# Building a pair-wise channel matrix with 64 block-diagonal products over 64 rows instead of 128 products over 16 rows

## The reference, cut to what matters

```python
def _L0_cond_ref(x, weights, condition):      # x (128, 64, 1024), weights (16, 64, 64)
    W = weights[condition]
    return jnp.einsum('bct,bcd->bdt', x, W)
...
x = x + _L0_cond_ref(x, L0_cond_weights, itok_B_0_15)
x = x + _L1_cond_ref(x, ..., itok_B_78_3631)   # long convolution along t, masked by a length
x = x + _L2_cond_ref(x, ..., itok_B_1_7)       # 1024x1024 linear layer along t, with adapters
x = x + _L3_cond_ref(x, ..., itok_B_8_3872)    # second long convolution
```

## Time and profile of the kernel before

| | us |
|---|---|
| median of 3 executions | 1711.64 (1707.01 to 1713.04) |
| the profiled execution | 1710.22 |
| its span in the trace | 1708.2 |
| PE busy | 1578.8 (92%) |
| first product of L561 | 10.79 |
| first product of stage 0 (L612) | 31.14 |

### The profile page before, as it was taken

One profiled execution on the slowest core, in us unless ns is written; L12 is line 12 of the kernel. 1 busy time (PEld: TensorE's weight loads), 2 busy tenths in 40 slices (PEclk: granted clock), 3 DMA queues, 4 the chain that ended last, 5 costly groups with the idle time before them and its releaser, 6 DMA issues.

```text
span 1708.2 us, 30846 instructions
## 1 busy us (share of the span) xinstructions
PE 1578.8 (92%) x12183; PEld 1033.3 (60%) x12183; DVE 1029.7 (60%) x1336; ACT 531.8 (31%) x674; POOL 826.4 (48%) x365
## 2 busy tenths in 40 slices
PE   6577774899999999999999999999999999999996
PEld 6576773365666656565657574747474747474744
DVE  6577766546575756565655656665656565656532
ACT  3444442323232323232323232323232323232211
POOL 2000006336556555656565656574747473838334
PEclk9888987899999999999999999999999999999998
DMA  4799994336263535353535252626252525252314
GB/s 120 195 334 368 356 342 159 74 48 160 48 147 60 140 66 135 71 135 71 135 70 136 61 145 52 149 47 148 58 140 66 140 66 140 66 128 74 79 50 99
DMA packets 433122, 216.80 MB, mean 127 GB/s; under 512 B 345336, under 2 KB 419584, under 8 KB 431040
## 3 DMA queue, kind: packets, MB, share of 16 engines
q1 hardware_dynamic: 413760, 204.19, 45.5%
q10 hardware_dynamic: 19328, 12.14, 2.5%
HBM read 94.19 MB, written 71.76 MB: 97 GB/s over the span
## 4 chain that ended last, share of the span: by engine, by line
PE 82%; DVE 6%; DMA 4%; issue 3%; SPq 2%; ACT 2%; ACTq 1%; POOL 0%; POOLq 0%; DVEq 0%
PE ps L730 39%; PE ps L765 7%; PE ps L668 7%; PE ps L695 6%; PE ps L722 5%; PE ps L738 5%; DMA arena<-in_x_dram 4%; PE ps L778 3%; PE ps L612 3%; PE ps L672 3%; PE ps L712 2%; PE ps L708 1%; SPq L352 1%; PE ps L561 1%; DVE arena L1462 1%
## 5 line engine op out<-in xcount | busy, mean ns | idle before, releaser
L730 PE MATMUL ps<-arena,w2t 128*128 128x512 f16 x3072 | 681.3, 379 | 0.0
L730 PEld LDWEIGHTS ps<-arena,w2t 128*128 128x128 f16 x3072 | 300.6, 98 | 362.5
L529 POOL TENSOR_TENSOR arena<-arena 128x1024 f32<-128x1024 f16 x64 | 152.8, 2387 | 545.8 <-DMA arena<-arena 528.2
L1468 DVE TENSOR_SCALAR arena<-ps,biasx 128x512 f32<-128x512 f32 x128 | 94.3, 747 | 214.6 <-ACT arena L1056 214.4
L1056 ACT ACTIVATE arena<-ps,biasx 128x512 f16<-128x512 f32 x128 | 87.3, 688 | 425.6 <-PE ps L738 425.6
L505 POOL TENSOR_TENSOR arena<-arena 128x1024 f32<-128x1024 f32 x32 | 73.7, 2305 | 288.6 <-DMA arena<-tab_scratch 261.3
L612 PE MATMUL ps<-arena 128*128 128x128 f32 x1024 | 150.2, 312 | 57.5 <-DMA arena<-in_x_dram 35.9
L612 PEld LDWEIGHTS ps<-arena 128*128 128x128 f32 x1024 | 141.3, 223 | 64.8 <-issue 33.8
L695 PE MATMUL ps<-arena 128*128 128x512 f16 (+1 forms) x768 | 138.7, 332 | 11.8 <-DVE arena L1389 9.4
L765 PE MATMUL ps<-arena 128*128 128x256 f16 (+1 forms) x1536 | 138.8, 247 | 3.2 <-DVE arena L1462 3.0
L532 POOL TENSOR_TENSOR arena<-arena,one_xs 128x1024 f32<-128x1024 f32 x64 | 136.1, 2126 | 5.0
(11 more groups left out here) (211 smaller groups left out, 2126.8 us busy)
## 6 DMA issues: line engine op xcount, KB each, us to landing
arena<-in_x_dram SPq DMA_DIRECT2D x64, 512.0 KB, 8.9
out_dram<-arena SPq DMA_DIRECT2D x64, 512.0 KB, 2.9
gbuf<-x_scratch SPq DMA_DIRECT2D x120, 256.0 KB, 3.6
x_scratch<-arena SPq DMA_DIRECT2D x16, 1024.0 KB, 11.6
arena<-krow_scratch SPq DMA_DIRECT2D x32, 512.0 KB, 4.4
x_scratch<-arena SPq DMA_DIRECT2D x16, 896.0 KB, 8.8
arena<-tab_scratch SPq DMA_DIRECT2D x32, 200.0 KB, 2.7
gbuf<-in_L_cond_weight_dram ACTq DMA_DIRECT2D x8, 512.0 KB, 8.4
```

The costliest lines, as they stand in the source:

```text
L529: nc.gpsimd.tensor_tensor(past[:, h % 2].rearrange("p (k t) -> p k t", k=NBLK), x3t[:, h % 2, 0], x3t[:, h % 2, 1], ALU.add).then_inc(past ...
L730: nc.tensor.matmul(ps[:, 4 + o % 3, :], w2t[:, part, k, o * P:(o + 1) * P], xx[:, :, k, :], start=(k == 0 and q == 0), stop=False)
L1468: ts(x3f[:, o % 2], ps[:, 4 + o % 3, :].rearrange("p (h b) -> p h b", h=HG), XS / FS, biasx[:, o:o + 1], ALU.mult, ALU.add).then_inc(s2_ou ...
```

## The change

The weights are loaded four times, each time whole (16 rows of 16 KB) and each time onto other partitions: copies 0 and 1 onto partitions 0 to 31 in the left 4096 columns of `w0n`, copies 2 and 3 onto partitions 32 to 63 in the right 4096 columns. The other two quarters of `w0n` are set to zero by VectorE, ahead of its first wait. `onehot` becomes 64 rows x 32 pairs: rows 0 to 31 are compared with the even samples' identifiers, rows 32 to 63 with those of the odd samples plus 32. Since identifiers are below 16, only copies 0 and 2 are ever picked. For a given d, one stationary matrix of 64 rows x 128 columns then holds the even samples' columns in its upper left and the odd samples' in its lower right quarter, and one product fills all 128 PSUM partitions.

```diff
-        w0n = area(56, 16)
+        w0n = area(56, 32)
...
-        onehot = sb("onehot", [NID, B], F32)
+        onehot = sb("onehot", [4 * NID, PAIRS], F32)
...
-            for quarter in range(4):
-                cols = slice(quarter * (C * C // 4), (quarter + 1) * (C * C // 4))
-                sp.dma_start(w0n[0:NID, cols], w0.rearrange("i c d -> i (c d)")[:, cols]).then_inc(w0_loaded, 16)
+            for copy in range(4):
+                q = copy // 2
+                sp.dma_start(w0n[NID * copy:NID * (copy + 1), q * C * C:(q + 1) * C * C],
+                             w0.rearrange("i c d -> i (c d)")).then_inc(w0_loaded, 16)
...
-            pe.wait_ge(w0_ready, 1)
-            src = w0n[0:NID, :].rearrange("i (c d) -> i d c", d=C)
+            pe.wait_ge(w0_ready, 2)
+            src = w0n[0:4 * NID, :].rearrange("i (m d) -> i d m", d=C)
             for dgroup in range(8):
                 for e in range(8):
-                    for q in range(2):
-                        mm = nc.tensor.matmul(ps[q * C:(q + 1) * C, dgroup, e * PAIRS:(e + 1) * PAIRS], src[:, 8 * dgroup + e, :],
-                                              onehot[:, :].rearrange("i (n q) -> i q n", q=2)[:, q, :], start=True, stop=True)
+                    mm = nc.tensor.matmul(ps[:, dgroup, e * PAIRS:(e + 1) * PAIRS], src[:, 8 * dgroup + e, :],
+                                          onehot[:, :], start=True, stop=True)
                 mm.then_inc(pick_summed, 1)
...
+            for q in range(2):
+                nc.vector.memset(w0n[2 * NID * q:2 * NID * (q + 1), (1 - q) * C * C:(2 - q) * C * C], 0.0)
             dve.wait_ge(iota_done, 3)
             dve.wait_ge(ids_loaded, 64)
             nc.vector.tensor_copy(idf[:, :, :], ids[:, :, :])
             link(nc.vector.tensor_copy(pcol, pcoli))
-            ts(onehot[:, :], idf[0:NID, 0, :], pcol[0:NID, :], None, ALU.is_equal)
+            pair_ids = idf[:, 0, :].rearrange("p (n q) -> p q n", q=2)
+            ts(onehot[0:2 * NID], pair_ids[0:2 * NID, 0], pcol[0:2 * NID, :], None, ALU.is_equal)
+            ts(onehot[2 * NID:4 * NID], pair_ids[2 * NID:4 * NID, 1], float(2 * NID), pcol[2 * NID:4 * NID, :], ALU.add, ALU.is_equal)
             dve.wait_ge(w0_loaded, 64)
-            diag = w0n[0:NID, 0:C * C]
-            diag = bass.AP(diag.tensor, diag.offset, [diag.ap[0], [C + 1, C]])
-            ts(diag, diag, 1.0, None, ALU.add).then_inc(w0_ready, 1)
+            for q in range(2):
+                own = w0n[2 * NID * q:2 * NID * (q + 1), q * C * C:(q + 1) * C * C]
+                own = bass.AP(own.tensor, own.offset, [own.ap[0], [C + 1, C]])
+                ts(own, own, 1.0, None, ALU.add).then_inc(w0_ready, 1)
```

## The result

The changed kernel takes 1724.74 us (median of 4 executions, 1722.5 to 1726.37) against 1709.43 us of the kernel before, timed with it (4 executions, 1707.01 to 1713.04). The ratio is 1.0087, with a 95% interval from 1.0062 to 1.0112: slower by 10.6 to 19.1 us. The prediction had 1716.3 us, 4.7 us above the kernel before, and a range that ended at 1721.

The account below looks back on a forecast made before the run. Bound: two nearly equal paths to stage 0, TensorE's products and VectorE's parameters. Weights 5.0 us late, 0.1 for additions, 0.4 won by products: stage 0 4.7 us later, 1711.64 + 4.7 = 1716.3 us; range 1709.5 to 1721.

Parts of the forecast that it names:

- The path to stage 0: Ahead of stage 0: TensorE's products and VectorE's parameter chain end within 0.2 us; faster products are worth 0.4 us.
- third view: ScalarE's timeline: it waits for VectorE's angles_ready at 23.86 us, so 5 us of TensorE's gain become idle time.
- 3.22 us of tables and functions: ScalarE's table loads, sine and tanh before group 5, all taken to follow angles_ready: 3.22 us.
- The products: TensorE's products ahead of stage 0: 128 records at 110 ns, 14 us in place of 19.08.
- the upper bound: TensorE's products: a record costs at most twice 74.5 ns if the stationary side sets it, 19.1 us in all.
- (d): TensorE's products stay the bound at 160 ns per record; stage 0 6.4 us later, 1718.0 us; chance 0.08.
- The weights: Weight loads ahead of VectorE's parameter chain: 1.05 MB at 130 GB/s land at 15.5 us, 5.0 us later than VectorE asked before.
- (a): Weight loads arrive at the full rate; only 0.6 us added, 1712.2 us; chance 0.15.
- The fills: Two VectorE fills ahead of its first wait: 5.4 to 8.2 us, hidden, cost 0.
- (b): VectorE's fills and GpSimd's work exclude each other; stage 0 8.1 us later, 1719.7 us; chance 0.13.
- (c): Denser products leave TensorE's clock at the upper level; stage 0's first 32 records save 2.9 us, 1713.4 us; chance 0.09.
- Carried to the end: Stage 0's 4.7 us delay passes unchanged through later layers to the end of the execution: median 1716.3 us.

Follow-up runs that it names:

- The run with 112.5 ns per record: Changed kernel with loads spread over 128 partitions, products over 128 rows with contiguous stationary columns, 27 identity products ahead: 1709.35 us against 1708.69 for the kernel before.
- the small kernel's products: Kernel before with the changed kernel's four weight loads, its own products reading copy 0 alone: 1714.30 us against 1708.35, ratio 1.0041.

## Why the prediction was wrong, point by point

**The path to stage 0** was read rightly in the main. Two paths end there within 0.2 us, and faster products alone bring little. The run with 112.5 ns per record shows it: its products are done at 26.12 us, 18.8 us earlier than in the changed kernel, and stage 0 begins at 30.14, 1.0 us earlier than before the change. TensorE idles 4.01 us in front of it, and the execution took 1709.35 us, against 1708.69 for the kernel before. A saving of 5 us and more on TensorE had become idle time, as the prediction's third view said. ScalarE's timeline in that run shows the other path, VectorE's parameters:

```profile
22.01 1.28 ACT L897 ACT_TABLE_LOAD   x1
24.55 0.31 ACT L897 ACTIVATE gbuf<-gbuf 128x128 f32<-128x128 f32 x1 [1.26 <-DVE gbuf L1174]
```

It shows a small miss too. The prediction put 3.22 us of tables and functions behind angles_ready, but the first table load (1.28 us) does not need the angles and runs ahead of the wait once TensorE is early. From the end of the instruction that carries angles_ready (24.53 us) to stage 0 it is 5.6 us here, not 6.9. So faster products would have been worth some 1.7 us and not 0.4; in the change itself TensorE was not early, and this played no part.

**The products** are the term that failed. The prediction put a record between 74.5 ns and twice that, 149, and took 110; it measured 219.6. The step in error is the upper bound. It took the 74.5 ns per record for the cost of one record, when it was the cost of one of two that ran beside each other, for the upper and the lower half of the output. Alone, a record with 64 columns costs 112 to 113 ns, so the bound had to be twice that, 225, and not 149. The sign of this was in the text: 128 columns in stage 0 cost 212 ns at first and 120 ns later, and the 110 taken lies below both, though the products run early. With 212 ns in its place the same sum gives 27.1 us for the products, an end at 42.9 us and stage 0 at 44.2; with the measured 28.1 us it gives 45.1, 14.0 of the 15.0 us by which stage 0 came later, and a median of 1725.6, against 1724.74 measured. So this one term carries the miss; the last 1.0 us is the products' later start, 16.78 for 15.8. The wrong width of the moving side (32 for 64) entered no term; 64 and 128 cost the same here, and 32 was not measured.

The rival that had the mechanism was (d), in which TensorE stays the bound. It had a chance of 0.08 and 160 ns, still too little, and was summed to 1718.0. Its mechanism held, at 219.6 ns.

**The weights** were right in mechanism and nearly in size: landing at 15.5 us was forecast, and VectorE's addition starts at 16.27. Rival (a), weights at the full rate, is out. The price of 6.0 us in stage 0's start with the small kernel's products (37.09 against 31.14) compares with the forecast 4.7. Ports shared by neighbouring partitions, which the prediction put in a sentence by itself, stood the test.

The Trainium skill's rule in "SBUF — State Buffer", section "Door 1: The DMA port swizzle", says that 16 neighbouring partitions reach 4 of the 16 ports. The run with every eighth partition agrees (11.7 us to landing became 7.3), as does the 112 GB/s of the changed kernel beside its 104.

**The fills** cost nothing, and rival (b) is out: GpSimd's clearing kept its place. But the cover was thinner than forecast. The fills began at 1.66 us and not at 0.7, stand 4.35 us apart from start to start (3.47 us each by the profile), and ended at 9.48, where the text expected before 9.

**The clock** (c) is not borne out: the first 32 records of stage 0 took 5.59 us instead of 6.78, but over all sixteen traces of stage 0 with all its rows they took 5.18 to 6.78 us (5.18 to 6.78 behind products of 64 columns, 5.51 to 6.70 behind those of 128), where the later rate gives 3.85. The 1.2 us cannot be put down to the change.

**Carried to the end.** The term added to the end as forecast. Starts of stage 0 and medians stand in one line: 31.14 us and 1708 to 1709, 37.09 us and 1714.3, 46.16 us and 1724.7. The chance given for slower by over 0.5% was 0.11, for (b) with dear fills or for (d) with the slowest landing. It was small because a record was held to be bounded near 149 to 160 ns; that the late weights and the products add on TensorE once it is the bound was in (d)'s sum.

## What to carry to other kernels

When a busy engine's mean per instruction is read from a stream, ask what ran beside it. Merging two half-width products into one of full width saves nothing if the halves already overlapped: here the stationary columns, and not the number of products, set the time (112 to 113 ns for 64 alone, 219.6 for 128, 149 for two times 64 side by side). Before an operation ahead of a critical stage is made cheaper, look for a second path of the same length, and charge the change for what it loads more, at the rate at which loads of that very shape moved. Copies that went onto neighbouring partitions were dear here (6 us); for the same bytes spread over all partitions VectorE did not wait at all.

## What the runs showed of the hardware that was not expected

- fp32 records with 64 stationary columns start 112 to 113 ns apart when nothing is beside them, and take 74.5 ns each when those for the two halves of the output are issued in turn.
- fp32 records with 128 stationary columns: 215 to 221 ns at the lower level of TensorE's clock for 16, 64 and 128 rows and for 64 and 128 moving columns. At the upper level 112.5 ns if the columns are contiguous, and no faster than at the lower if they lie 64 or 256 bytes apart.
- During products with 16 or 64 rows the granted clock fell from 1.00 to 0.50 in three kernels, and stage 0 with 64 rows took 225 ns per record still at 49 us; it fell too during products over 128 rows with a step. Products over 128 rows with contiguous columns ran at the upper rate for all of their 14.4 us.
- Fills of 4096 columns on VectorE (3.47 us) and of 8192 on GpSimd (6.92 us) ran at the same time and did not hold each other up, while a conversion on VectorE ended only with GpSimd's fill, whether it began at 7.73 (2.51 us) or at 9.50 us (0.74 us).
